# Ordering the 128 partitions of layer 1's tiles channel first in a two-layer convolution kernel

## The chip, the cores and the metric

The kernel runs on one core of one Trainium2 chip. The metric is device microseconds (us) of one execution, the median of several runs. A core has a matrix engine (PE; its weight loads are written PEld), a vector engine (DVE), an activation engine (ACT), a general engine (POOL) and a queue that issues transfers (SP). Each runs its own instruction stream in order and waits on semaphores that the others raise. Transfers (DMA) are issued by SP here and carried by 16 DMA engines.

## What is computed

Two layers on a batch of 32 images of 96 channels, 56 by 56 pixels. Layer 0 is a 7x7 depthwise convolution, a layer norm over channels, a two-layer MLP with GELU and a residual; the change leaves it alone. Layer 1, cut to what matters:

```python
x = conv5x5_depthwise(x) + conv_b;  xs = silu(x)               # (B, 96, L), L = 56*56
dts, Bs, Cs = split(einsum('kd,bdl->bkl', x_proj_w, xs))       # 6, 4 and 4 rows
delta = softplus(einsum('dr,brl->bdl', dt_w, dts) + dt_b)
log_dA = maximum(delta * -exp(A_logs), log(1e-9))              # for each of N = 4 states
P = exp(cumsum(log_dA, axis=-1))
hs = P * cumsum(delta * Bs * xs / maximum(P, 1e-9), axis=-1)
y = einsum('bdnl,bnl->bdl', hs, Cs) + xs * Ds
```

## The kernel before

The images are worked in 8 groups of `GI` = 4. Layer 0 runs over all groups and stores its result in `x1`; then layer 1 runs over them. In layer 1 a tile of 128 partitions holds 4 images by `CB` = 32 channels, and three tiles (t = 0, 1, 2) hold the 96 channels of a group. The pixels of an image are cut into 7 bands of `BT` = 448. A group has 7 bands x 3 tiles x 4 states = 84 steps s. In each step DVE runs two scans along the pixels (`scan_q` L1082, `scan_h` L1109) with a product between them (`gate`, L1098), POOL makes `u` (`times_b`, L1000) and `h` times C (`times_c`, L1010 and L1013), ACT makes `d_a` for five steps ahead (L1189, L1195), and PE adds the result to the bank `ps_y` (`add_y`, L1380). The first of the four states of a tile is preceded by the product of `xs` and `skip` (L1377), which opens `ps_y` anew.

All through the group the front of the next group is worked between these steps, one unit at a time: "turn" (PE turns a strip of `x1pad`, L1300), "conv" (PE multiplies windows with the banded filter in `taps`, L1307) and "back" (PE turns `conv` back so that channels and images are the partitions, L1320). ACT keeps each unit's bank: `keep_front`, L1145, into `win` or `conv`, and `silus`, L1152, into `xs`. The front of a group has 192/8 = 24 conv units, each with one filter load `taps` of 672 KB. ACT's copies for one conv unit write 4 channels x 4 images x 28 row pairs to 112 partitions of `conv`.

When a tile's four states are in `ps_y`, ACT copies them to `y` (`keep_y`, L1215), at step 4k + 6, and SP stores `y` to the output (`store`, L932) at step 4k + 7. There is one tile `y` and one bank `ps_y`. So `keep_y` waits for the tile's last product on PE and for the whole landing of the store before (`y_stored`), and PE's L1377 of the next tile waits for `keep_y`:

```python
act.wait_ge(y_added, g * S + (r + 1) * N + H_SLOTS)
act.wait_ge(y_stored, (g * RUNS + r + 1) * 16)
nc.scalar.activation(y[:, :], ps_y[:, 0:BT], ACT.Copy).then_inc(y_kept, 1)
```

SP's order is written out in `group`: for each step first the loads due in 5 steps (`load_slab` L906 into `x1pad`, `load_taps` L915, each of which waits until PE is done with its slot), then the store. Also on each other's way are `spread_b` (PE, L1350) and `keep_b` (ACT, L1203), which make `b_rows` of the next band in steps 6 to 10 of a band, `softplus` (ACT, last part L1171), and `sum_delta` (DVE, L1072), which waits for it. `lay_out` on the host orders the weights that go with the partitions.

Of the kernel before, what the change touches and what calls it, by code (L numbers as in the profile page):

```python
# [28 lines left out]
ds = bass.ds  # L29

IMAGES, C, H, W = 32, 96, 56, 56
L = H * W
GI = 4
# [37 lines left out]
CB = 32  # L71
# [648 lines left out]
def layer1(nc, groups, x1, t2, consts, out):  # L720

    x1img = x1.rearrange("r (h w) -> r h w", h=H)
    with ExitStack() as ctx:  # L723
        def sb(name, shape, dt=F32):
            return ctx.enter_context(nc.sbuf_tensor(name, shape, dt))
# [23 lines left out]
        conv = sb("conv2", [TOK, IMG_BLK, GI * C])  # L749
# [139 lines left out]
        @block.sync  # L889
        def _(sp):  # L890
            sp.dma_start(ident[:, :], consts["ident"]).then_inc(ident_in, 16)
            small = [(xproj[:, :, :], consts["xproj"]),
                     (xs[:, 0, 0:2 * 128], consts["sel"]),
                     (xs[:, 1, 0:TILES * 128], consts["dtw"]),
                     (ds_col[:, :], consts["ds"]),
                     (conv_bias[:, :], consts["cb2"]), (low_rows[:, :], consts["low_rows"]),
                     (a_neg[:, :, :], consts["a_logs"])]

            def load_slab(f, first, k):

                if k >= SLABS:
                    sp.wait_ge(front_done, f * FRONT + turn_unit[k - SLABS] + 1)
                elif not first:
                    sp.wait_ge(front_done, (f - 1) * FRONT + turn_unit[k - SLABS] + 1)
                rows = slice(CB * (k % SLABS), CB * (k % SLABS) + CB)
                sp.dma_start(xpad[rows, PAD2:PAD2 + H, PAD2:PAD2 + W],  # L906
                             x1img[ds((f * GI + k % GI) * C + CB * (k // GI), CB), :, :]
                             ).then_inc(slab_ready[k % SLABS], 16)

            def load_taps(f, first, k):  # L910
                if k >= SLOTS2:
                    sp.wait_ge(front_done, f * FRONT + conv_unit[k - SLOTS2] + 1)
                elif not first:
                    sp.wait_ge(front_done, (f - 1) * FRONT + conv_unit[k - SLOTS2] + 1)
                sp.dma_start(taps[k % SLOTS2][:, :, :, :], t2[k]).then_inc(taps_ready[k % SLOTS2], 16)  # L915


            loads = [(load_slab, k, turn_unit[k] - TURNS2 + 1) for k in range(CBS * GI)]
            loads += [(load_taps, k, conv_unit[k]) for k in range(QUNITS)]
            loads.sort(key=lambda load: load[2])  # L920

            sp.wait_ge(xpad_zero, BORDERS)
            for n, (load, k, _) in enumerate(loads):
                if n == SLABS:
                    for dst, src in small:
                        sp.dma_start(dst, src).then_inc(consts_in, 16)
                load(0, True, k)

            def store(g, r):
                b, t = r // TILES, r % TILES  # L930
                sp.wait_ge(y_kept, g * RUNS + r + 2)
                sp.dma_start(out.rearrange("(i c) l -> i c l", c=C)[ds(g * GI, GI), t * CB:(t + 1) * CB,  # L932
                                                                    b * BT:(b + 1) * BT],
                             y[:, :]).then_inc(y_stored, 16)

            def first_slabs(f):
                for load, k, _ in loads[:SLABS]:
                    load(f, False, k)

            def group(g, ahead):  # L940

                todo = loads[SLABS:] if ahead else []
                for s in range(S):
                    if ahead == 2 and s == S - 2 * STEPS:
                        first_slabs(g + 2)
                    while todo and unit_step[todo[0][2]] <= s + AHEAD:
                        load, k, _ = todo.pop(0)
                        load(g + 1, False, k)
                    if s >= N + Y_LAG + 1 and (s - N - Y_LAG - 1) % N == 0:
                        store(g, (s - N - Y_LAG - 1) // N)  # L950
                store(g, RUNS - 1)

            if last:
                first_slabs(1)
            if last > 1:
                with sp.Fori(0, last - 1) as g:
                    group(g, 2)
            if last:
                group(last - 1, 1)
            group(last, 0)  # L960
            sp.wait_ge(y_stored, (groups * RUNS + 1) * 16)
# [171 lines left out]
        def _(act):  # L1133
            def keep_front(f, i):

                kind, cb, k, p = units[i]
                act.wait_ge(front_done, f * FRONT + i + 1)
                if kind == "turn":
                    src = bank[i][0:WIN2, 0:TW2 * CB].rearrange("p (w c) -> p w c", c=CB)
                    dst = win[cb % 2][:, :, k, p * TW2:(p + 1) * TW2].rearrange("p c w -> p w c")  # L1140
                else:
                    src = bank[i][0:TOK, 0:CQ * BLOCKS].rearrange("p (c i b) -> p c i b", c=CQ, i=GI)
                    dst = conv[:, :, cb * 128:(cb + 1) * 128].rearrange("p b (i c) -> p c i b",
                                                                        i=GI)[:, k * CQ:(k + 1) * CQ, :, :]
                nc.scalar.activation(dst, src, ACT.Copy).then_inc(front_kept, 1)  # L1145

# [107 lines left out]
            for i in range(EARLY):  # L1254
                if units[i][0] != "back":
                    keep_front(0, i)
                elif units[i - 1][0] != "back":
                    silus(0, next(burst for burst in backs if i in burst))
# [181 lines left out]
def banded(w, k):  # L1440

    cols = W + k - 1
    kt = (ROWS + k - 1) // ROWS
    t = np.zeros((C, kt * ROWS, cols, ROWS, W), np.float32)
    for o in range(ROWS):
        for j in range(W):
            t[:, o:o + k, j:j + k, o, j] = w
    t = t.reshape(QUNITS, CQ, kt, ROWS * cols, TOK).transpose(0, 3, 1, 2, 4)
    return np.pad(t, ((0, 0), (0, 128 - ROWS * cols), (0, 0), (0, 0), (0, 0)))


def lay_out(i):

    image, channel = np.divmod(np.arange(128), CB)

    def rows(a):

        a = a.reshape((TILES, CB) + a.shape[1:]).swapaxes(0, 1)
        return np.ascontiguousarray(np.tile(a, (GI,) + (1,) * (a.ndim - 1)))

    xproj = np.zeros((128, TILES, XD), np.float32)
    dtw = np.zeros((XD, TILES, 128), np.float32)
    sel = np.zeros((XD, 2, 128), np.float32)
    low_rows = np.zeros((XD, 2), np.float32)
    low_rows[ONE, 1] = 1
    weights = i["L1_conv_x_proj_w"]
    for part in range(2):
        for t in range(TILES):
            for p in range(128):
                m, c = image[p], t * CB + channel[p]  # L1470
                for n in range(N):
                    for k in range(2):
                        row = n * XB + (2 * part + k) * GI + m
                        xproj[p, t, row] = weights[R + k * N + n, c]
                        sel[row, k, p] = 1
                        low_rows[row, 0] = part
                dts = m * XB + DT0 + part * R
                xproj[p, t, dts:dts + R] = weights[:R, c]
                dtw[dts:dts + R, t, p] = i["L1_conv_dt_w"][c]
                low_rows[dts:dts + R, 0] = part  # L1480
                dtw[ONE, t, p] = i["L1_conv_dt_b"][c]
    return {
        "x": i["x"], "t1": banded(i["L0_conv_conv_w"][:, 0], K1), "ident": np.eye(128, dtype=np.float32),
        "w1": i["L0_conv_w1"], "w2": i["L0_conv_w2"], "b1": np.ascontiguousarray(i["L0_conv_b1"].reshape(FT, 128).T), "b2": i["L0_conv_b2"],
        "ln_g": i["L0_conv_ln_g"], "ln_b": i["L0_conv_ln_b"], "ls": i["L0_conv_layer_scale"].reshape(C),
        "cb1": i["L0_conv_conv_b"],
        "t2": banded(i["L1_conv_conv_w"][:, 0], K2),
        "xproj": xproj, "dtw": dtw.reshape(XD, -1), "sel": sel.reshape(XD, -1), "low_rows": low_rows,
        "ds": rows(i["L1_conv_Ds"]), "cb2": rows(i["L1_conv_conv_b"]),
        "a_logs": rows(i["L1_conv_A_logs"]),  # L1490
    }

# [19 lines left out]
```

## Time and profile before

| | us |
|---|---|
| median of 3 runs (4328.0 to 4345.21) | 4344.35 |
| the profiled execution | 4339.02 |
| its span on the core | 4337.2 |
| layer 1, from its first loads at 1845 | 2492 |

The profile is one execution of the program. Busy time of an engine says how long it worked; a wait names the instruction that waited and the one whose semaphore ended the wait. `PEclk` is the clock granted to the matrix engine: 1.00 is 2.4 GHz and 0.50 is 1.2 GHz. In the timeline a row gives the start, the duration, the engine, the line and the tiles, and in brackets the idle time of the engine ahead of it with what ended it. Buffer numbers are left out of the tiles' names.

### The profile page before, as it was taken

The numbers are of one execution on the slowest core, as the hardware profiler recorded it, in microseconds if no ns is written. First come the engines' busy times: TensorE is split into PE (matmuls) and PEld (weight loads), VectorE is DVE, ScalarE is ACT, GpSimd is POOL, SyncE is SP. The second block draws the span as 40 slices with busy tenths as digits, with TensorE's granted clock in tenths as the row PEclk, the third lists the DMA queues.
The fourth block names the chain that finished last, engine by engine and source line by source line (L and its number), as shares of the span: only waits on it lengthen the run. The fifth ranks groups of instructions, "written<-read, shape, count | busy, mean of one in ns | idle before, by whom it ended". The sixth has DMA issues, their size and how long they took to land. (4 is left out here: it accounts for less than half of the span.)

```text
span 4337.2 us, 74817 instructions
## 1 busy us (share of the span) xinstructions
PE 3832.3 (88%) x22806; PEld 2788.2 (64%) x22806; DVE 3180.4 (73%) x4643; ACT 2788.1 (64%) x4796; POOL 2363.8 (55%) x2504
## 2 busy tenths in 40 slices
PE   7999999999999999977888889888888888898777
PEld 6787888878787878675555545545545555455432
DVE  3767667676758585705977978878878778788898
ACT  1545445453637272747877877878778778778875
POOL 0323223232314141405877868777868778777798
PEclk9999999999999999988997978979979979889977
DMA  7565555546464744274423324424324334243100
GB/s 233 146 181 155 168 165 155 174 136 193 120 213 99 237 101 165 74 186 90 107 73 92 103 55 108 109 56 104 102 59 109 81 78 112 62 102 97 39 20 22
DMA packets 314885, 507.50 MB, mean 117 GB/s; under 512 B 190000, under 2 KB 255248, under 8 KB 314144
## 3 DMA queue, kind: packets, MB, share of 16 engines
q1 hardware_dynamic: 314432, 502.08, 42.3%
q8 instruction: 209, 3.42, 0.3%
q14 instruction: 244, 2.00, 0.2%
HBM read 424.94 MB, written 77.07 MB: 116 GB/s over the span
## 5 line engine op out<-in xcount | busy, mean ns | idle before, releaser
L522 ACT ACTIVATE act_h<-ps_up,b 128x448 f32<-128x448 f32 x672 | 408.4, 633 | 789.1 <-PE ps_up L640 788.9
L1013 POOL TENSOR_TENSOR h<-h,c_rows 128x448 f32<-128x448 f32 x672 | 762.9, 1135 | 103.8 <-ACT c_rows L1210 53.3
L319 POOL TENSOR_TENSOR h_low<-act_h,h_high 128x448 fp32r<-128x448 f32 x224 | 287.2, 1282 | 902.0 <-ACT h_high L527 901.9
L1000 POOL TENSOR_TENSOR u<-dxs,b_rows 128x448 f32<-128x448 f32 x672 | 763.9, 1137 | 27.0 <-ACT b_rows L1203 20.4
L1380 PE MATMUL ps_y<-h,ident 128*128 128x448 f32 x1344 | 725.5, 627 | 42.5 <-POOL h L1013 32.1
L1082 DVE TENSOR_TENSOR_SCAN ps_q<-d_a,q_last,ps_q 128x448 f32<-128x448 f32 x576 | 659.6, 1145 | 25.2 <-ACT d_a L1195 25.2
L1109 DVE TENSOR_TENSOR_SCAN h<-d_a,h_last,ps_q 128x448 f32<-128x448 f32 x576 | 645.7, 1121 | 9.7 <-PE ps_y L1380 9.6
L1307 PEld LDWEIGHTS ps_front<-win,taps 120*112 120x112 f32 x4608 | 537.8, 188 | 137.5 <-issue 136.5
L613 PE MATMUL ps_stage<-win,taps 124*112 124x112 f32 x6144 | 607.9, 260 | 2.7 <-DVE w_low L366 2.7
L613 PEld LDWEIGHTS ps_stage<-win,taps 124*112 124x112 f32 x6144 | 607.7, 178 | 3.3 <-DVE w_low L366 2.8
L1307 PE MATMUL ps_front<-win,taps 120*112 120x112 f32 x4608 | 550.1, 273 | 5.4 <-ACT win L1145 3.7
L1098 DVE SCALAR_TENSOR_TENSOR ps_q<-ps_q,u 128x448 f32<-128x448 f32 x672 | 422.4, 629 | 160.7 <-POOL u L1000 137.3
L1189 ACT ACTIVATE d_a<-delta,log_eps,a_neg 128x448 f32<-128x448 f32 x672 | 505.5, 753 | 50.0 <-DVE h L1109 33.1
L314 POOL TENSOR_TENSOR ln_rstd<-ln_var,minus_half 112x7 f32<-112x7 f32 x128 | 244.7, 1912 | 406.8 <-DVE ln_var L401 406.8
L429 DVE TENSOR_TENSOR conv<-ps_stage,bias_row 112x448 f32<-112x448 f32 x192 | 180.0, 937 | 350.2 <-PE ps_stage L613 350.2
L1380 PEld LDWEIGHTS ps_y<-h,ident 128*128 128x128 f32 x1344 | 249.0, 209 | 243.7 <-issue 168.6
L1195 ACT ACTIVATE d_a<-d_a 128x448 f32<-128x448 f32 x672 | 384.5, 573 | 2.7
L1377 PE MATMUL ps_y<-xs,skip 128*128 128x448 f32 x336 | 196.6, 672 | 194.0 <-ACT y L1215 193.6
L1072 DVE SCALAR_TENSOR_TENSOR delta<-ps_prep,z_log 128x448 f32<-128x448 f32 x168 | 104.2, 620 | 293.0 <-ACT z_log L1171 289.1
L1145 ACT ACTIVATE conv<-ps_front 112x448 f32<-112x448 f32 x192 | 181.8, 947 | 173.8 <-PE ps_front L1307 173.6
L636 PE MATMUL ps_up<-hn_high,w_high 96*128 96x448 f32 x672 | 254.6, 379 | 35.2 <-DVE hn_low L411 20.3
L1300 PEld LDWEIGHTS ps_front<-ident,x1pad 32*120 32x120 f32 x2880 | 209.0, 151 | 116.9 <-issue 115.3
(93 smaller groups left out, 7118.2 us busy)
## 6 DMA issues: line engine op xcount, KB each, us to landing
taps<-in_t_dram SPq DMA_DIRECT2D x192, 896.0 KB, 5.2
taps<-in_t_dram SPq DMA_DIRECT2D x192, 672.0 KB, 4.8
xres<-in_x_dram SPq DMA_DIRECT2D x224, 168.0 KB, 2.5
x_dram<-x1o SPq DMA_DIRECT2D x224, 168.0 KB, 2.0
x1pad<-x_dram SPq DMA_DIRECT2D x96, 392.0 KB, 8.0
out_dram<-y SPq DMA_DIRECT2D x168, 224.0 KB
xpad<-in_x_dram SPq DMA_DIRECT2D x29, 1176.0 KB, 10.6
conv<-in_x_dram SPq DMA_DIRECT2D x3, 1176.0 KB, 15.3
```

Source lines behind the costliest of these rows:

```text
L319: nc.gpsimd.tensor_tensor(h_low[u % 2][:, 1, :], act_h[u % 2][:, 1, :], h_high[u % 2][:, 1, :], ALU.subtract).then_inc(h_low_ready[1], 1)
L522: nc.scalar.activation(act_h[u % 2][:, t, :], ps_up[t][:, 0:BT], ACT.Gelu, bias=b1[:, t:t + 1]).then_inc(gelu_done, 1)
L613: mm = nc.tensor.matmul(ps_stage[q % 2][0:TOK, c * BLOCKS:(c + 1) * BLOCKS], taps[q % SLOTS1][0:WIN1, c, k, :], win[:, q * CQ + c, :, k:k ...
L1000: nc.gpsimd.tensor_tensor(u[s % U_SLOTS][:, :], dxs[:, t, :], b_rows[n][:, :], ALU.mult).then_inc(u_done, 1)
L1013: nc.gpsimd.tensor_tensor(h[s % H_SLOTS][:, :], h[s % H_SLOTS][:, :], c_rows[n][:, :], ALU.mult).then_inc(hc_done, 1)
L1082: nc.vector.tensor_tensor_scan(ps_q[s % 2][:, 0:BT], d_a[s % DA_SLOTS][:, :], no_q.broadcast_to([128, BT]), first, ALU.mult, ALU.add).then ...
L1098: nc.vector.scalar_tensor_tensor(ps_q[s % 2][:, 0:BT], ps_q[s % 2][:, 0:BT], 1.0, u[s % U_SLOTS][:, :], ALU.min, ALU.mult).then_inc(gated, 1)
L1109: nc.vector.tensor_tensor_scan(h[s % H_SLOTS][:, :], d_a[s % DA_SLOTS][:, :], ps_q[s % 2][:, 0:BT], first, ALU.mult, ALU.add).then_inc(h_d ...
L1189: nc.scalar.activation(d_a[s % DA_SLOTS][:, :], delta[:, t, :], ACT.Relu, bias=log_eps[:, 0:1], scale=a_neg[:, t, n:n + 1]).then_inc(clipp ...
L1195: nc.scalar.activation(d_a[s % DA_SLOTS][:, :], d_a[s % DA_SLOTS][:, :], ACT.Exp, bias=LOG_EPS).then_inc(d_a_ready, 1)
L1307: mm = nc.tensor.matmul(bank[i][0:TOK, c * BLOCKS:(c + 1) * BLOCKS], taps[n % SLOTS2][0:WIN2, c, w, :], win[cb % 2][:, k * CQ + c, :, w:w ...
L1380: nc.tensor.matmul(ps_y[:, 0:BT], ident[:, :], h[s % H_SLOTS][:, :], start=False, stop=(n == N - 1)).then_inc(y_added, 1)
```

## The change

The 128 partitions of a layer 1 tile were ordered image first (partition = 32 image + channel); now channel first (partition = 4 channel + image). ACT's copy L1145 writes `conv` in that order, the host lays the weights out to match, and the store of `y` has 32 leading entries (channels) of 4 images in place of 4 leading entries (images) of 32 channels. The store's source is the same `y[:, :]` of 128 partitions, its pieces are the same 448 pixels (1,792 bytes), and it moves the same 224 KB.

```diff
             def store(g, r):
                 b, t = r // TILES, r % TILES
                 sp.wait_ge(y_kept, g * RUNS + r + 2)
-                sp.dma_start(out.rearrange("(i c) l -> i c l", c=C)[ds(g * GI, GI), t * CB:(t + 1) * CB,
+                sp.dma_start(out.rearrange("(i c) l -> c i l", c=C)[t * CB:(t + 1) * CB, ds(g * GI, GI),
                                                                     b * BT:(b + 1) * BT],
                              y[:, :]).then_inc(y_stored, 16)
...
-                    dst = conv[:, :, cb * 128:(cb + 1) * 128].rearrange("p b (i c) -> p c i b",
+                    dst = conv[:, :, cb * 128:(cb + 1) * 128].rearrange("p b (c i) -> p c i b",
                                                                         i=GI)[:, k * CQ:(k + 1) * CQ, :, :]
...
-    image, channel = np.divmod(np.arange(128), CB)
+    channel, image = np.divmod(np.arange(128), GI)
...
-        return np.ascontiguousarray(np.tile(a, (GI,) + (1,) * (a.ndim - 1)))
+        return np.ascontiguousarray(np.repeat(a, GI, axis=0))
```

No instruction is added, taken away or moved on any engine. On SP, at steps 61 to 67 of a group (sixth band), the queue stood as follows before; `taps2_0` to `taps2_2` are the three slots of the filter tile, `ISA` and `REGISTER_ALU` are address and semaphore work.

```order
L915 DMA taps2_0<-in_t2_dram 128x1344
L912 REGISTER_ALU
L915 DMA taps2_1<-in_t2_dram 128x1344
L931 REGISTER_ALU
L932 ISA
L932 DMA out_dram<-y 4x32x448
L912 REGISTER_ALU
L915 DMA taps2_2<-in_t2_dram 128x1344
```

The same place in the changed kernel:

```order
L915 DMA taps2_1<-in_t2_dram 128x1344
L931 REGISTER_ALU
L932 ISA
L932 DMA out_dram<-y 32x4x448
L912 REGISTER_ALU
```

The order is the same; only the shape of the store has moved from 4x32x448 to 32x4x448. On ACT the copy of a conv unit changes its shape and nothing else:

```order
-L1145 ACTIVATE conv<-ps_front 112x4x4x28
+L1145 ACTIVATE conv<-ps_front 112x16x28
```

Channels and images, apart before, now lie next to each other in `conv` and fold into 16; the innermost 28 row pairs are 384 elements apart in both.

## Rows read from the trace of the kernel before

**Rows 1.** The page, part 1: busy time, share of the span, instructions.

```profile
PE 3832.3 (88%) x22806; PEld 2788.2 (64%) x22806; DVE 3180.4 (73%) x4643; ACT 2788.1 (64%) x4796; POOL 2363.8 (55%) x2504
```

**Rows 2.** Waits, 2010 to 4130 us: waiting <- releaser: total us, times, longest.

```profile
PE ps_y L1377 <- ACT y L1215: 164.4, 135, 3.8
...
ACT y L1215 <- DMA out_dram<-y: 11.6, 7, 2.2
```

**Rows 3.** Timeline of steps 61 to 68 of the third group: start, duration, instruction.

```profile
2811.02 6.68 SPq L915 DMA_DIRECT2D taps<-in_t_dram  x2
2817.95 0.64 SPq L932 DMA_DIRECT2D out_dram<-y  x1
...
2824.68 0.54 ACT L1215 ACTIVATE y<-ps_y 128x448 f32<-128x448 f32 x1 [1.73 <-DMA out_dram<-y]
...
2825.36 1.83 PE L1377 MATMUL ps_y<-xs,skip 128*128 128x448 f32 x2 [3.31 <-ACT y L1215]
...
2830.86 0.56 PE L1350 MATMUL ps_bc<-parts,sel 32*128 32x448 f32 x1
...
2831.46 0.54 ACT L1203 ACTIVATE b_rows<-ps_bc 128x448 f32<-128x448 f32 x1 [4.08 <-PE ps_bc L1350]
...
2832.16 1.14 POOL L1000 TENSOR_TENSOR u<-dxs,b_rows 128x448 f32<-128x448 f32 x1 [0.79 <-ACT b_rows L1203]
...
2833.12 0.62 DVE L1072 SCALAR_TENSOR_TENSOR delta<-ps_prep,z_log 128x448 f32<-128x448 f32 x1 [5.20 <-ACT z_log L1171]
...
2835.92 0.19 POOL L1010 TENSOR_TENSOR h_last<-h,zeros 128x1 f32<-128x1 f32 x1 [2.62 <-DVE h L1109]
```

**Rows 4.** Timeline of ACT: the first and the last of the seven waits.

```profile
2226.18 0.54 ACT L1215 ACTIVATE y<-ps_y 128x448 f32<-128x448 f32 x1 [2.09 <-DMA out_dram<-y]
...
4025.21 0.54 ACT L1215 ACTIVATE y<-ps_y 128x448 f32<-128x448 f32 x1 [0.78 <-DMA out_dram<-y]
```

**Rows 5.** Timeline of POOL behind the first and the last wait.

```profile
2236.36 0.19 POOL L1010 TENSOR_TENSOR h_last<-h,zeros 128x1 f32<-128x1 f32 x1 [2.62 <-DVE h L1109]
...
4035.34 0.19 POOL L1010 TENSOR_TENSOR h_last<-h,zeros 128x1 f32<-128x1 f32 x1 [1.34 <-DVE h L1109]
```

**Rows 6.** Windows: from:to, length, busy of PE, PEld, DVE, ACT, POOL, PEclk, DMA share, GB/s.

```profile
2825.00:2831.00 6.00, 5.64 (x17) 3.80 (x17) 2.89 (x5) 2.35 (x5) 5.84 (x8) 0.50 0.17 49
2840.00:2850.00 10.00, 7.78 (x44) 5.38 (x45) 10.00 (x12) 7.54 (x13) 9.81 (x10) 1.00 0.09 23
4025.00:4031.00 6.00, 5.10 (x18) 3.14 (x19) 4.33 (x7) 2.79 (x6) 5.84 (x8) 0.72 0.37 130
```

**Rows 7.** Timeline of PE at two shorter stalls.

```profile
2868.21 1.02 PE L1377 MATMUL ps_y<-xs,skip 128*128 128x448 f32 x2 [1.45 <-ACT y L1215]
...
3168.71 1.59 PE L1377 MATMUL ps_y<-xs,skip 128*128 128x448 f32 x2 [1.46 <-ACT y L1215]
```

**Rows 8.** Windows, the 5 us behind each of these two stalls.

```profile
2868.20:2873.20 5.00, 4.96 (x13) 2.11 (x13) 5.00 (x7) 4.79 (x10) 5.00 (x6) 1.00 0.18 48
3168.70:3173.70 5.00, 4.99 (x9) 1.94 (x9) 5.00 (x7) 3.20 (x7) 5.00 (x6) 0.66 0.18 48
```

**Rows 9.** DMA issues: count, KB each, median us from issue to landing.

```profile
x_dram<-x1o SPq DMA_DIRECT2D x224, 168.0 KB, 2.0
x1pad<-x_dram SPq DMA_DIRECT2D x96, 392.0 KB, 8.0
```

**Rows 10.** SP's own waits, 4300 to 4338 us: for the last store, once issued.

```profile
SPq L723 <- DMA out_dram<-y: 4.6, 1, 4.6
```

**Rows 11.** DMA packets, 4322 to 4331 us: one store of `y` alone, and 8 KB instructions.

```profile
DMA packets 133, 0.24 MB, mean 26 GB/s; under 512 B 4, under 2 KB 132, under 8 KB 132
```

**Rows 12.** DMA packets, 1843 to 1847 us: one store of `x1o` and one load.

```profile
DMA packets 256, 0.24 MB, mean 59 GB/s; under 512 B 32, under 2 KB 256, under 8 KB 256
```

**Rows 13.** Groups of ACT by form, 2010 to 4130 us: busy us, mean ns, idle before.

```profile
L1145 ACT ACTIVATE win<-ps_front 120x480 f32<-120x480 f32 x167 | 178.1, 1066 | 114.9 <-PE ps_front L1300 114.9
L1145 ACT ACTIVATE conv<-ps_front 112x448 f32<-112x448 f32 x168 | 159.1, 947 | 130.5 <-PE ps_front L1307 130.3
```

## The prediction, on record before the changed kernel ran

> **What bounds the kernel now.** I read the page's busy times first: PE is busy 88% of the span, DVE 73% [rows 1]. No engine is full, so a shorter transfer pays only where somebody waits for it and where that somebody holds up the rest. The change touches one transfer, the store of `y`, and one ACT copy. So the second view is the list of waits over the steady part of layer 1. PE waits 164.4 us for ACT's copy of `y`, in 135 places; ACT itself waits for the store of `y` in 7 places, 11.6 us together [rows 2]. The first number looks large, but it is mostly ACT's own order of work. Only the 11.6 us are the store's.
>
> There are seven groups with a next group to prepare, and each has one such wait, at its 67th step: the first is 2.09 us, the last 0.78 [rows 4]. The timeline of the third shows how it comes about [rows 3]. SP issues two filter loads ahead of the store, and the second had to wait for PE, so the store goes out at 2817.95, behind 672 KB just issued. It lands at 2824.68, where ACT's copy can start 1.73 us late. PE has been idle 3.31 us by then.
>
> **Whom that holds up.** Behind PE's stall come the two products into `ps_y`, a conv unit, and then the product L1350 at 2830.86. ACT had waited 4.08 us for it to make `b_rows`. The same ACT stream makes `z_log`, for which DVE had waited 5.20 us, and POOL, which had work stored up, runs dry last: 0.79 us for `b_rows` and 2.62 us for DVE's scan [rows 3]. A little later DVE and POOL are full, 10.00 and 9.81 of 10 us from 2840 on [rows 6], and PE is not. So PE is on the path through the stall, and POOL's idle time, 3.41 us here, is what a quicker PE could give back at most. Behind the seven waits these sums are 2.62, 3.68, 3.41, 3.65, 3.25, 3.23 and 1.34 us, 21.2 together (third in [rows 3], first and last in [rows 5]).
>
> **The clock.** A stall costs PE more than its length. In the 6 us after the stall the granted clock is 0.50, that is 1.2 GHz; behind the last one, where PE stood for 2.37 us, it is 0.72, a mix of both levels [rows 6]. The first pair of products takes 1.83 us after the stall [rows 3] and 1.02 where the clock held [rows 7]. Without the wait for the store all seven stalls would be 1.6 us long (3.31 less 1.73 here). The trace has two stalls nearly that long at another step: 1.45 us, after which the clock stayed at 1.00, and 1.46 us, after which it was 0.66 over 5 us [rows 7, 8]. At 1.6 us both can happen.
>
> **The store.** How many DMA engines carry it can be counted. A transfer ends with small packets that raise the semaphore. The last stores of the program lie alone: 128 packets of data and 4 below 512 bytes [rows 11]. In the other window a store of `x1o` (96 rows) and a load of 128 rows of 512 bytes leave 256 - 96 - 128 = 32 small ones, 16 each [rows 12]. So the store of `y` runs on 4 engines and the others on 16. With 32 leading entries I expect 16. What 32 entries do is not in this trace in so many packets.
>
> The Trainium skill ("DMA: Bandwidth & Descriptors", section on why a DMA increments its semaphore by 16) says that the number of engines is the largest up to 16 that divides the slowest dimension of both sides; for 4 against 128 that gives 4, as the trace has it, and for 32 against 128 it gives 16. By that rule the change does what it says.
>
> Price: SP waited 4.6 us for the last store [rows 10]. The nearest transfer on 16 engines is that of `x1o`, 2.0 us for 168 KB [rows 9]. For 224 KB the bounds are 2.0 (all of it fixed) and 2.7 (2.0 x 224/168, all of it by size), so a store lands 1.9 to 2.6 us earlier. Each engine then has 8 rows instead of 32 behind the filter load. I take 2.2.
>
> **The sum, part by part.**
> - End of the program: nothing hides the last store, 2.2 us less.
> - The waits of ACT: three of the seven are above 1.9 us (2.09, 2.17, 2.09). At 2.2 saved all 11.6 go; at 1.9, 11.0. In the other stores nobody waits for the landing, and they give nothing: ACT does not come back before four steps, some 14 us.
> - The clock behind the stalls. If every place became like the last one, with the short low clock and no wait (POOL would still idle 1.34 - 0.78 = 0.56 us there), the seven give 21.2 - 7 x 0.56 = 17.3 us, the 11.6 included. If the clock stays as it is, 11.6. If it never falls, all of POOL's idle time, 21.2.
> - The ACT copy into `conv`: 947 ns for 448 elements. The copy into `win`, also with no two neighbours written in turn, takes 1066 ns for 480, 2.2 ns an element against 2.1 [rows 13]. Innermost are 28 elements 384 apart before and after; only the outer steps swap. I take nothing. The bounds are 30 ns either way, 168 x 0.03 = 5 us if all of it lay on the path, about half of it in truth, since ACT idles 130.5 us ahead of these copies.
> - Loads: a filter or `x1pad` load behind a store comes in earlier on four engines, but the list of waits has none of PE for a load in this stretch. Nothing. PE's products sum the same values over permuted partitions: same shapes, nothing.
> - SP: issue of the store takes 0.64 us [rows 3]; SP has slack, nothing.
>
> Forecast: 17.3 less 0.5 for what stays of the longest waits, and 2.2 at the end: 19 us. The profiled execution took 4339.0, so it becomes 4320. It lies 5.3 us under the median of the runs, 4344.35; the same 19 us from there give **4325 us**, 0.44% less. About 0.5% (21.7 us) is what a measurement of this kernel can tell from no change.
>
> **The rivals.**
> 1. *The clock falls as before.* A stall of 1.6 us still brings the full low stretch. Then 11.3 + 2.2 = 13.5 us: 4331. For it: the stall of 1.46 us was already enough once [rows 8]. Against: 2.37 us brought a shorter stretch than 3.31 [rows 6].
> 2. *The clock never falls there.* 21.2 - 0.5 + 2.2 = 23 us: 4321. For it: the stall of 1.45 us [rows 7, 8]. Against: 1.6 is longer.
> 3. *Nothing moves.* The store stays on 4 engines, or its landing at these seven places is set by the filter loads ahead of it on all engines, so that it comes no earlier. 4342 to 4344. For it: the store goes out right behind 672 KB [rows 3]. Against: engines work their own share in order, and a quarter of the rows on each is less behind the same load.
> 4. *Slower.* An engine's rows, neighbouring channels 12.5 KB apart in the output before, are now four images 1.2 MB apart. If such writes are slow, the store lands later. The nearest transfer of scattered pieces, `x1pad` with 8.0 us [rows 9], is 3.4 us above 4.6. Then each of the seven waits grows by 3.4 and so does the end: 8 x 3.4 = 27 us, 4371. It decides from no gain at all per store; the 0.5% are reached at 2.7 us more per store. Against: most of the 8.0 us are 1,792 small pieces, and a store of `y` has 128.
>
> On that the Trainium skill ("DMA: Bandwidth & Descriptors", section on latency and other measured facts) lists that copies whose rows lie 2, 4 or 8 MiB apart, powers of two, run at down to half the rate, and that a pitch off by 4 KiB restores it. Here the pitch is 1,204,224 bytes, no power of two; by that page the store would not suffer, and no run so far shows it.
>
> **How the numbers follow.** Forecast 0.38, rival 1 0.20, rival 2 0.18, nothing 0.12, slower 0.07; 0.05 for a larger gain, if the groups' falls of the clock elsewhere shift in our favour. The three runs before lie 17 us apart, so each case has some 8 us about it. The range 4308 to 4345 takes in the cases from the larger gain to no effect, and leaves out rival 4 and the far tails. Faster by over 0.5% holds rival 2 in good part, the larger gain and the better side of the forecast: 0.33. Within 0.5%: 0.59. Slower: 0.08.
>
> **What would show each step.** The lone store at the end: 16 small packets, not 4, and SP's last wait 2.0 to 2.7 us. The wait of ACT for the store: gone, or a few tenths in three places. PE's stalls at these steps: 1.6 us each; the clock in the 6 us behind them at 0.7 or above (0.5 speaks for rival 1, 1.0 for rival 2). POOL's idle time there: about 0.6 us. The period of a group, 300 us between two such copies, goes to 297.5. The copy into `conv`: 947 ns still. The forecast is wrong if POOL or DVE turns out to be held by something else behind the stall, if the copy's time moves by more than 30 ns, or if the store does not come in earlier.

## The result

| | median us | runs |
|---|---|---|
| before | 4344.78 | 4328.0 to 4349.79 |
| changed kernel | 4284.92 | 4279.36 to 4288.19 |

The ratio is 0.9867 with a 95% interval from 0.9846 to 0.9889: 60 us less where 19 were forecast, and below the range of 4308 to 4345. The profiled execution took 4279.36 us, against 4339.02 before.

The transfer itself did what was expected. The lone store of `y` near the end, from the DMA packets of the changed kernel between 4262 and 4272 us (before: [rows 11]), and SP's own last wait (before: [rows 10]):

```profile
DMA packets 146, 0.25 MB, mean 25 GB/s; under 512 B 16, under 2 KB 144, under 8 KB 144
```

```profile
SPq L723 <- DMA out_dram<-y: 1.8, 1, 1.8
```

16 small packets close the store instead of 4: it runs on 16 engines. SP waits 1.8 us for the last one instead of 4.6, a little less than the 2.0 to 2.7 that I had given. The page's list of DMA issues (count, KB, median us to landing; [rows 9] answers to the second line) shows that the loads land earlier too; the filter loads took 4.8 us before:

```profile
taps<-in_t_dram SPq DMA_DIRECT2D x192, 672.0 KB, 4.0
x1pad<-x_dram SPq DMA_DIRECT2D x96, 392.0 KB, 5.3
out_dram<-y SPq DMA_DIRECT2D x168, 224.0 KB, 2.4
```

ACT's waits at `keep_y` fell from 11.6 us in 7 places [rows 2] to this line of the view of L1215 (what ended ACT's idle time, us, times):

```profile
  DMA out_dram<-y: 0.2, 1
```

**Where the 60 us arise.** The starts of ACT's copies of `y` mark the steps of each group. Cut at steps 14, 58 and 74, the fourth group reads so in the windows of the kernel before (columns as in [rows 6]):

```profile
2949.60:3089.70 140.10, 124.07 (x763) 82.89 (x762) 126.99 (x186) 119.04 (x206) 119.85 (x145) 0.99 0.41 105
3089.70:3159.80 70.10, 60.05 (x296) 40.92 (x296) 51.70 (x71) 51.54 (x86) 44.70 (x53) 0.85 0.34 81
3159.80:3249.90 90.10, 76.88 (x313) 42.15 (x312) 65.31 (x92) 64.39 (x110) 64.62 (x71) 0.73 0.28 69
```

and in the changed kernel:

```profile
2927.70:3067.80 140.10, 124.10 (x763) 82.92 (x762) 127.24 (x188) 119.04 (x206) 119.83 (x145) 0.99 0.38 105
3067.80:3131.50 63.70, 55.50 (x298) 37.88 (x298) 51.14 (x70) 51.20 (x87) 44.55 (x53) 0.95 0.38 89
3131.50:3214.40 82.90, 67.59 (x312) 36.34 (x310) 65.53 (x90) 63.66 (x110) 64.55 (x72) 0.81 0.29 75
```

The long first stretch is the same to the tenth. DVE, ACT and POOL have the same work in all three. In the second stretch (steps 58 to 74, the *site* of the wait) 6.4 us are gone, and in the third (step 74 to step 14 of the next group, the *turn*) 7.2. In both the granted clock is higher, 0.95 for 0.85 and 0.81 for 0.73, and PE's busy time shorter with the same matmuls. Over the seven groups the sites take 450.6 us instead of 486.3, 36 less. The turns of the first six take 515.3 instead of 542.6, 27 less. The end gives 3, and 6 are lost again in the seventh turn, the middles and the first steps.

Within the site the fourth group reads as follows, cut at the copies of `y` at steps 62, 66, 70 and 74, before:

```profile
3112.10:3125.40 13.30, 9.61 (x63) 7.30 (x62) 6.71 (x11) 9.93 (x18) 10.29 (x13) 0.97 0.52 166
3125.40:3140.40 15.00, 13.91 (x64) 9.51 (x64) 9.46 (x15) 10.97 (x21) 11.03 (x15) 0.80 0.07 22
3140.40:3159.80 19.40, 16.78 (x74) 10.62 (x74) 16.86 (x21) 15.27 (x25) 11.15 (x11) 0.82 0.05 13
```

and after:

```profile
3090.10:3101.10 11.00, 9.60 (x63) 7.30 (x62) 4.45 (x7) 9.70 (x18) 8.08 (x10) 1.00 0.46 152
3101.10:3113.50 12.40, 11.30 (x64) 7.87 (x64) 11.69 (x18) 10.97 (x21) 12.09 (x16) 1.00 0.19 70
3113.50:3131.50 18.00, 14.77 (x76) 9.23 (x76) 16.29 (x20) 15.01 (x26) 12.12 (x13) 1.00 0.04 14
```

The wait itself gives 2.3 us. The stretches behind it, where the clock now holds at 2.4 GHz, are 2.6 and 1.4 us shorter. (The 0.95 of the whole site comes from steps 58 to 62, where the clock is 0.85 in both kernels.) PE's stall in the fourth group before, and the timeline of the changed kernel at the place of [rows 3], one group on:

```profile
3126.10 1.83 PE L1377 MATMUL ps_y<-xs,skip 128*128 128x448 f32 x2 [3.68 <-ACT y L1215]
```

```profile
3096.31 0.62 SPq L932 DMA_DIRECT2D out_dram<-y  x1
...
3101.12 0.57 ACT L1215 ACTIVATE y<-ps_y 128x448 f32<-128x448 f32 x1
...
3101.83 0.99 PE L1377 MATMUL ps_y<-xs,skip 128*128 128x448 f32 x2 [1.41 <-ACT y L1215]
...
3105.19 0.54 ACT L1203 ACTIVATE b_rows<-ps_bc 128x448 f32<-128x448 f32 x1 [1.35 <-PE ps_bc L1350]
...
3106.85 0.62 DVE L1072 SCALAR_TENSOR_TENSOR delta<-ps_prep,z_log 128x448 f32<-128x448 f32 x1 [0.57 <-ACT z_log L1171]
```

PE stands for 1.41 us instead of 3.68 and its pair takes 0.99 instead of 1.83 us. DVE's wait is 0.57 instead of 5.44, and POOL does not idle there any more. Six of the seven groups look like this one. In the first, PE still stands for 1.83 us, the clock behind it is 0.72 and the site takes 68.3 us.

### The profile page after: what moved, and what is told of

Same layout as the page of the kernel before. It is cut to its first block and busy times, and to the rows that moved or that the text cites. A ratio compares the mean times of both kernels' runs of the same rounds, so it can differ in the third digit from the quotient of the medians.

```text
span 4277.6 us, 74817 instructions
## 1 busy us (share of the span) xinstructions
PE 3785.7 (89%) x22806; PEld 2758.0 (64%) x22806; DVE 3180.8 (74%) x4643; ACT 2783.8 (65%) x4796; POOL 2363.1 (55%) x2504
## 5 line engine op out<-in xcount | busy, mean ns | idle before, releaser
L1307 PEld LDWEIGHTS ps_front<-win,taps 120*112 120x112 f32 x4608 | 527.1, 185 | 134.4 <-issue 132.6
L1307 PE MATMUL ps_front<-win,taps 120*112 120x112 f32 x4608 | 539.5, 269 | 6.1 <-ACT win L1145 3.7
L1145 ACT ACTIVATE conv<-ps_front 112x448 f32<-112x448 f32 x192 | 181.7, 946 | 166.0 <-PE ps_front L1307 165.8
```

Source lines behind the costliest of these rows:

```text
L1307: mm = nc.tensor.matmul(bank[i][0:TOK, c * BLOCKS:(c + 1) * BLOCKS], taps[n % SLOTS2][0:WIN2, c, w, :], win[cb % 2][:, k * CQ + c, :, w:w ...
```

## The experiments

The theory after the result: the shorter landing of the store takes away ACT's wait at step 66; that keeps PE's stall so short that its clock holds, and most of the gain is the clock. Rivals: the order of partitions itself brings the gain; or the relief of four DMA engines, by earlier loads; or each us of wait simply costs a us; and for the turn, that its gain is not the store's at all. The table gives medians, beside the kernel before on the same chip, and the site and turn of the profiled execution (mean of seven sites, range of the first six turns).

| kernel | us | before | ratio, 95% interval | site us | turns us |
|---|---|---|---|---|---|
| changed kernel | 4284.9 | 4344.8 | 0.9867 (0.9846 to 0.9889) | 64.4 | 82.9 to 89.4 |
| img_4x16 | 4295.7 | 4339.9 | 0.9889 (0.987 to 0.9909) | 64.3 | 83.0 to 90.5 |
| img_2x2 | 4336.2 | 4339.9 | 0.999 (0.9976 to 1.0004) | 70.6 | 83.2 to 91.2 |
| store_first | 4276.3 | 4339.9 | 0.984 (0.9823 to 0.9856) | 64.3 | 83.0 to 90.4 |
| chan_4x8 | 4284.2 | 4339.9 | 0.9868 (0.9836 to 0.99) | 63.8 | 82.8 to 90.5 |
| delay66_4 | 4283.6 | 4347.7 | 0.9847 (0.9808 to 0.9887) | 63.7 | 87.2 to 90.8 |
| delay66_8 | 4310.6 | 4347.7 | 0.9918 (0.9888 to 0.9948) | 66.8 | 83.1 to 90.7 |
| delay66_12 | 4322.2 | 4341.4 | 0.9955 (0.9939 to 0.997) | 66.1 | 90.2 to 90.4 |
| delay30_8 | 4271.9 | 4347.7 | 0.9831 (0.9801 to 0.986) | 63.5 | 82.9 to 90.2 |
| delay74_2 | 4286.5 | 4341.4 | 0.9875 (0.9844 to 0.9906) | 64.7 | 82.7 to 90.3 |
| before_d74_1 | 4346.3 | 4338.5 | 1.0006 (0.9987 to 1.0026) | 68.7 | 90.2 to 90.4 |
| before_d74_3 | 4339.7 | 4338.5 | 1.0008 (0.9997 to 1.0019) | 68.6 | 83.0 to 90.2 |
| before_d74_6 | 4335.1 | 4338.5 | 0.9999 (0.998 to 1.0018) | 69.1 | 83.1 to 90.8 |
| before_y_first | 4255.6 | 4341.4 | 0.9793 (0.9762 to 0.9823) | 66.6 | 80.0 to 82.5 |
| y_before_front | 4225.1 | 4347.7 | 0.9727 (0.9693 to 0.9761) | 64.3 | 77.6 to 82.6 |
| both_first | 4206.4 | 4341.4 | 0.9689 (0.9661 to 0.9718) | 61.7 | 79.7 to 83.3 |

The kernel before has 69.5 and 90.1 to 90.9 in these columns. Its own medians lie up to 9 us apart between these sets of runs, so kernels of different rows are best compared by their ratios.

### Layout or landing: img_4x16

Image first as before, with four transfers per store:

```diff
-                sp.dma_start(out.rearrange("(i c) l -> i c l", c=C)[ds(g * GI, GI), t * CB:(t + 1) * CB,
-                                                                    b * BT:(b + 1) * BT],
-                             y[:, :]).then_inc(y_stored, 16)
+                for i in range(GI):
+                    sp.dma_start(out[ds((g * GI + i) * C + t * CB, CB), b * BT:(b + 1) * BT],
+                                 y[i * CB:(i + 1) * CB, :]).then_inc(y_stored, 16)
```

> The kernel before with its image-first partitions, but each store of y issued as four transfers, one per image, each with 32 leading entries. Theory S (the shorter landing of the store makes the difference, by way of ACT's wait at the 67th step and PE's clock behind it): small packets per store 64, all 16 engines busy; landing 1.5 us after that of the changed kernel because of three more issues of 0.55 us; ACT's waits for the store nearly gone; 4285 us, give or take 8. Theory L (the channel-first order itself makes it, by ACT's copy or the weights): 4345.

4295.7 us, with the sites at 64.3 us. The page's issues (columns as above):

```profile
out_dram<-y SPq DMA_DIRECT2D x672, 56.0 KB, 1.6
```

So most of the gain is there without the new order of partitions: 44 us of 60, and at the sites all of it. Its ratio, 0.9889, is not clear of the 0.9867 of the changed kernel, since the intervals overlap. What its profiled execution lacks lies at the turns and in the first steps. The order of partitions is only the means by which one transfer gets 32 leading entries.

### Eight engines: chan_4x8

The changed kernel, with four transfers of 8 channels each:

```diff
-                sp.dma_start(out.rearrange("(i c) l -> c i l", c=C)[t * CB:(t + 1) * CB, ds(g * GI, GI),
-                                                                    b * BT:(b + 1) * BT],
-                             y[:, :]).then_inc(y_stored, 16)
+                for k in range(4):
+                    sp.dma_start(out.rearrange("(i c) l -> c i l", c=C)[t * CB + 8 * k:t * CB + 8 * k + 8,
+                                                                        ds(g * GI, GI), b * BT:(b + 1) * BT],
+                                 y[32 * k:32 * k + 32, :]).then_inc(y_stored, 16)
```

> The changed kernel with its channel-first partitions, but each store of y issued as four transfers of 8 channels, with 8 leading entries each, so that 16 rows lie on each of 8 engines. Theory S: landing between before and after (0.6 us more than on 16 engines, 1.7 us more for the issues); ACT's waits 0 to 3 us in all; 4285 to 4300. Theory L: 4285.

4284.2, the changed kernel's time. ACT's waits for the store:

```profile
ACT y L1216 <- DMA out_dram<-y: 0.7, 2, 0.4
```

Half the engines do as well as all, since nobody waits for the rest of the landing. This run does not tell the theories apart by itself; with img_4x16 it says that any landing short enough at step 66 will do.

### Two engines: img_2x2

```diff
+                for k in range(2):
+                    sp.dma_start(out.rearrange("(i c) l -> i c l", c=C)[ds(g * GI + 2 * k, 2), t * CB:(t + 1) * CB,
+                                                                        b * BT:(b + 1) * BT],
+                                 y[64 * k:64 * k + 64, :]).then_inc(y_stored, 16)
```

> The kernel before, but each store of y issued as two transfers of two images, with 2 leading entries each, so that 64 rows lie on each of two engines instead of 32 on each of four. Theory S: a store lands some 2.4 us later still than before (32 more rows of 74 ns, read off the lone store's rows); ACT's waits for it grow from 11.6 us to 28 or more, and the time goes up by 10 to 40 us, 4355 to 4385. Theory L, or that the landing is of no matter: 4345.

The waits grew as said, but the time did not: 4336.2, within the noise of before. ACT's waits, and PE's stall in the fourth group:

```profile
ACT y L1216 <- DMA out_dram<-y: 30.5, 12, 4.2
```

```profile
3111.46 1.83 PE L1378 MATMUL ps_y<-xs,skip 128*128 128x448 f32 x2 [5.83 <-ACT y L1216]
```

A miss of my forecast, and the clearest sign against "a us of wait costs a us": of the 19 us more of waiting some 15 lie at the seven sites, and they lengthen them by 8 us together (3.4 are one wait at the end of a group), and the turns, 83 to 91 us, give that back. Behind stalls of 4.7 to 5.8 us the clock of the next 6 us is 0.65 to 0.74, where it was 0.50 to 0.56 behind five of the seven stalls of before; so the longer stall is in part paid back right behind it.

### The wait alone: store_first

Four leading entries as before; only SP's list is turned:

```diff
+                    if s >= N + Y_LAG + 1 and (s - N - Y_LAG - 1) % N == 0:
+                        store(g, (s - N - Y_LAG - 1) // N)
                     while todo and unit_step[todo[0][2]] <= s + AHEAD:
                         load, k, _ = todo.pop(0)
                         load(g + 1, False, k)
-                    if s >= N + Y_LAG + 1 and (s - N - Y_LAG - 1) % N == 0:
-                        store(g, (s - N - Y_LAG - 1) // N)
```

> The kernel before with 4 leading entries, but in SP's list the store of a step stands ahead of the loads of that step. No transfer is quicker; the store of the 64th step is issued some 5.6 us earlier, since it no longer waits behind a filter load. Theory S in the form that only the wait matters: ACT's waits for the store are gone, 4285 give or take 10. If instead the relief of the four engines is what counts (filter and image loads landing earlier), the time stays at 4345, and their landings stay at 4.8 and 8.0 us.

4276.3, no slower than the changed kernel, with loads that land later than in any other kernel but img_2x2 (6.1 and 8.7 us), and PE's stall in the fourth group:

```profile
taps<-in_t_dram SPq DMA_DIRECT2D x192, 672.0 KB, 6.1
x1pad<-x_dram SPq DMA_DIRECT2D x96, 392.0 KB, 8.7
```

```profile
3105.43 0.99 PE L1377 MATMUL ps_y<-xs,skip 128*128 128x448 f32 x2 [1.42 <-ACT y L1215]
```

This settles it between the wait and the load on the four engines. The quick landing is not needed; it is enough that the store does not stand behind a filter load on SP.

### Putting the wait back: delay66_4, delay66_8, delay66_12

The changed kernel with n tiny copies ahead of the copy of `y` at step 66. One takes about 0.18 us, but they overlap: four take 0.43 us in all, eight 0.82 and twelve 1.19. With eight:

```diff
+                    if more and s == 66:
+                        for k in range(8):
+                            nc.scalar.activation(ps_bc[:, BT + 8 * k:BT + 8 * k + 8], skip[:, 0, 0:8], ACT.Copy)
```

> The changed kernel with four of the tiny ACT copies at step 66, some 0.8 us. Theory C: PE's stall is 2.2 us, as long as the shortest of before; the clock falls behind it, 4300 to 4330. Theory linear: 7 x 0.8 = 6 us, 4291.

> The changed kernel with eight tiny ACT copies (8 elements each, some 0.2 us, into unused columns of a bank) ahead of the copy of y at step 66 of every group but the last. They stand in for the wait for the store: no transfer is touched. Theory C (the wait costs mostly by what PE's clock does behind it, there and at the turn of the group): most of the 60 us come back, 4325 to 4345, PE's stall 3 us and the granted clock 0.5 to 0.7 in the 6 us behind it. Theory linear (a us of wait costs a us): 7 x 1.6 = 11 us, 4296.

> The changed kernel with twelve tiny ACT copies (5 elements each) at step 66, where eight had brought PE's stall from 1.41 to 2.12 us and a fall of the clock behind it. Theory C: the stall is 2.8 us and the clock low for longer; the stretch from step 58 to 74 takes 69 to 70 us as in the kernel before (63.7 in the changed one, 66.9 with eight), and the whole 4310 to 4345. Theory linear: 66.9 plus 0.7.

The timelines of PE in the fourth group, in this order, with the window of the 6 us behind it for each:

```profile
3102.68 0.99 PE L1380 MATMUL ps_y<-xs,skip 128*128 128x448 f32 x2 [1.74 <-ACT y L1215]
```

```profile
3103.00:3109.00 6.00, 6.00 (x35) 4.07 (x34) 5.04 (x9) 4.63 (x10) 5.84 (x8) 1.00 0.24 96
```

```profile
3109.03 1.70 PE L1380 MATMUL ps_y<-xs,skip 128*128 128x448 f32 x2 [2.12 <-ACT y L1215]
```

```profile
3109.00:3115.00 6.00, 5.96 (x21) 3.61 (x22) 3.71 (x7) 2.94 (x7) 5.84 (x8) 0.72 0.21 81
```

```profile
3107.35 1.83 PE L1380 MATMUL ps_y<-xs,skip 128*128 128x448 f32 x2 [2.49 <-ACT y L1215]
```

```profile
3107.40:3113.40 6.00, 6.00 (x24) 3.62 (x25) 3.28 (x5) 3.08 (x7) 5.84 (x8) 0.74 0.15 59
```

The stall of 1.74 us costs nothing: the clock stays at 1.00 in all seven groups, and the median is that of the changed kernel. The stall of 2.12 us, 0.4 longer, brings the clock down in all seven: each site takes 3.1 us more than with 1.74, the whole 27 us more. With 2.49 us it is 4322, still 19 us below before. No transfer was touched, so an ACT delay alone brings back about 26 and 37 of the 60 us by the medians, 22 and 38 by the ratios. The three medians move by steps, not in proportion to the delay. Expected sizes were off: the copies add less to the stall than I had reckoned (0.33, 0.71 and 1.08 us), four cost less than either theory said, eight gave less than "most of the 60", and the site did not reach 69 us with twelve. Nor does the loss lie only at the sites: with twelve copies the seven sites give back 12 us, and the first six turns, 90.3 us each, all 27.

### Another place: delay30_8

The same eight copies at step 30.

> The changed kernel with the eight tiny ACT copies ahead of the copy of y at step 30 instead, the same step of a band three bands earlier, where PE is as busy. Theory C for any place: PE's stall there is 2.7 us, the clock falls behind it, 4310 to 4345. Theory linear or that only step 66 is tender: 4285 to 4296.

4271.9, 13 us *below* the changed kernel, though the intervals of the two ratios overlap. PE's stall at step 30 in the first and in the fourth group:

```profile
2102.61 1.86 PE L1380 MATMUL ps_y<-xs,skip 128*128 128x448 f32 x2 [2.06 <-ACT y L1215]
```

```profile
2973.47 1.02 PE L1380 MATMUL ps_y<-xs,skip 128*128 128x448 f32 x2 [2.05 <-ACT y L1215]
```

Without the copies this stall is 1.26 to 1.28 us long, so the eight bring it to 2.05 to 2.07 us, not to the 2.7 that I had reckoned with. Behind it the clock stays at 1.00 in six groups and falls to 0.73 in the first. The middle stretch takes 140.1 or 140.2 us in those six, no more than without the copies, so 0.8 us more of stall cost nothing there. Whether step 66 is more tender than step 30 is not shown by this: the stall here is shorter than the 2.12 us at which the clock fell in every group.

### The turns: delay74_2 and three kernels on the old store

One to six tiny copies at step 74, in the changed kernel (2) and in the kernel before (1, 3, 6), where the wait for the store is left as it was:

```diff
+                    if more and s == 74:
+                        for k in range(3):
+                            nc.scalar.activation(idle[:, 3 * k:3 * k + 3], skip[:, 0, 0:3], ACT.Copy)
```

> The changed kernel with two tiny ACT copies (8 elements, 0.3 us together) at step 74, where the turn of the group begins. Theory C for the turn (its time, 83 to 90 us from step 74 to step 14 of the next group, hangs on where PE's idle times fall against the steps of its clock, and not on the store): the turns take 83 to 90 us in another order than in the changed kernel, and the median lies anywhere from 4265 to 4300. If the turn's gain comes from the store: 83 to 88 us as before it, 4285.

> The kernel before, store and all, with one tiny ACT copy (3 elements, 0.18 us) at step 74, where the turn of the group begins. Question: the changed kernel's turns (step 74 to step 14 of the next group) take 83 to 89 us, those of the kernel before 90 us each time. Theory P (the turn depends on where its idle times fall against the clock, and the kernel before is caught in one pattern): turns leave 90 us in some groups, and the time is 0 to 30 us below before though work was added. Theory T (the turn is longer because of the wait at step 66 or the store): turns of 90 us, 4341 to 4345.

> The kernel before with three tiny ACT copies (0.5 us) at step 74. Theory P: turns anywhere from 83 to 91 us, 4305 to 4345. Theory T: turns of 90 us, 4345.

> The kernel before with six tiny ACT copies (1.1 us) at step 74. Theory P: turns anywhere from 83 to 91 us, 4305 to 4350. Theory T: turns of 90 us and 7 us more in all, 4350.

Medians of 4286.5, and of 4346.3, 4339.7 and 4335.1 against 4338.5: on average nothing moved. In delay74_2 the turns take 82.7 to 90.3 us in another order than in the changed kernel, as theory C for the turn has it. With one copy in the kernel before they stay at 90.2 to 90.4 us, as theory T has it. But the profiled execution of before_d74_3, the fastest of its eleven (4312.7), has two neighbouring groups whose turns are short. Windows, turn of the second group, then middle, site and turn of the third:

```profile
2550.60:2633.60 83.00, 67.40 (x311) 36.35 (x310) 65.18 (x90) 63.70 (x111) 64.43 (x71) 0.81 0.31 74
2633.60:2773.80 140.20, 124.18 (x763) 82.95 (x762) 127.34 (x188) 119.12 (x207) 119.93 (x145) 0.99 0.41 105
2773.80:2843.70 69.90, 60.08 (x296) 41.02 (x296) 51.64 (x70) 51.94 (x90) 44.69 (x53) 0.85 0.33 81
2843.70:2927.20 83.50, 68.54 (x313) 36.67 (x312) 64.98 (x91) 63.73 (x110) 64.43 (x71) 0.82 0.31 74
```

A site with the full wait, 69.9 us, is followed by a turn of 83.5. So a short turn does not need the store's wait gone (theory T falls in its strict form), and store_first has a turn of 90.4 without the wait. Yet the two are not independent. Over the first six groups of the fourteen profiled kernels that keep ACT's order, the turn takes 89.0 us on average behind the 26 sites longer than 69 us, 88.2 behind 21 sites of 65 to 68.5, and 86.4 behind the 37 shorter ones. That would be 2.6 x 6 = 16 us of the 27. It is a comparison across kernels and no test: delay66_4 has short sites and turns of 89.1 us in the mean. The medians say more. All five kernels in which PE's stall at step 66 stays short, and which are alike otherwise (changed, img_4x16, chan_4x8, store_first, delay66_4), lie 44 to 64 us below the kernel before, more than the 38 us that sites and end give; the three with copies at step 74 and the old store lie within 8 us of it. So more than the sites' share comes with the short stall at step 66. How it gets from step 66 to the turn, and which idle time decides between a turn of 83, 86, 88 or 90 us, stays open.

### A version that beats both: y_before_front, before_y_first, both_first

PE's waits for ACT's copy of `y` were still 151.8 us. In `group` of ACT the copy of `y` now stands ahead of the front's copy:

```diff
+                    if s >= N + Y_LAG and (s - N - Y_LAG) % N == 0:
+                        keep_y(g, (s - N - Y_LAG) // N)
                     if more:
                         for i in kept_at[s]:
                             keep_front(g + 1, i)
-                    if s >= N + Y_LAG and (s - N - Y_LAG) % N == 0:
-                        keep_y(g, (s - N - Y_LAG) // N)
```

> The changed kernel with ACT's copy of y ahead of the copy of the front unit's bank in the same step, so that PE gets ps_y back about 1 us earlier (the copy of a conv unit takes 0.95 us). Theory C: PE's stalls at L1377, 1.1 to 2.0 us each and 152 us in all, shrink by half, and with the shortest idle stretches gone the clock holds: 4200 to 4260. Against: the copy of y can then wait for PE's last product and hold up the front's bank, or POOL is the bound in these steps: 4275 to 4295.

> The kernel before (image first, stores on 4 engines) with ACT's copy of y ahead of the copy of the front's bank. It is due earlier, so it runs into the store before more often: the wait at step 66 grows by the 0.95 us of the conv unit's copy, to 2 to 3 us, and the clock falls behind it. 4290 to 4310, 65 to 85 us above the same edit on the changed kernel (4225). If the store's landing did not matter, it would come to 4225 as well.

> The changed kernel with both orders turned: on ACT the copy of y ahead of the front's copy, on SP the store ahead of the loads of its step. The first alone gave 4225. With the store issued up to 6 us earlier at step 64, no wait for it is left there either: 4205 to 4225. If none was left already: 4225.

The first is that edit on the changed kernel (4225.1), the second on the kernel before (4255.6), the third has store_first's edit besides (4206.4, a ratio of 0.9689, interval 0.9661 to 0.9718: 78 us below the changed kernel by the medians). The waits of the second and of the first, in this order:

```profile
PE ps_y L1377 <- ACT y L1215: 106.9, 98, 3.7
...
ACT y L1215 <- DMA out_dram<-y: 16.3, 7, 2.9
```

```profile
PE ps_y L1377 <- ACT y L1215: 100.5, 101, 2.9
...
ACT y L1215 <- DMA out_dram<-y: 6.0, 7, 1.8
```

The first falls in the range that I had given for it, but not in the way that theory C had it. PE's waits went from 151.8 to 100.5 us, a third less and not half. Nor does the clock hold better: over the whole execution it is 0.925, against 0.927 in the changed kernel. Its profiled execution has shorter middles (18 us in seven) and shorter turns (33 us in six), and sites of the same length.

`keep_y` comes earlier, so it meets the store again: 6.0 us even on 16 engines, none with the store issued first. The old store costs 30 us against the new one here, where I had expected 65 to 85. PE's stalls at step 66 with the old store are 2.5 to 3.7 us long, about as before, but the clock of the 6 us behind them is 0.72 to 0.74 in all seven groups and not down to 0.50; with the new store it is 0.72 in two groups and 1.00 in five. Why the same stall costs less clock here stays open. both_first came out at the lower end of what was expected.

## Why the prediction was wrong

**Right.** The chain [rows 3, 4] was the right one. The store moved from 4 to 16 engines; rival 3 falls, as does rival 4, with a landing of 2.4 us. The rule on the number of engines in the Trainium skill ("DMA: Bandwidth & Descriptors", section on why a DMA increments its semaphore by 16) gave 16 for 32 against 128 entries, and the 16 small packets agree. ACT's waits went from 11.6 to 0.2 us. The last wait of SP shrank by 2.8 us for the 2.2 taken. The copy into `conv` takes 946 ns in the mean for 947. The engines' work and the middle of the groups did not move.

**The stall.** I took 1.6 us for what would remain of PE's stall, from 3.31 less 1.73. It is 1.41, because ACT's copies overlap by about 0.2 us when nothing lies between them (in the fourth group the copy of the conv unit ends at 3101.31 and that of `y` starts at 3101.12), which the wait had hidden. At 1.6 I let both outcomes of the clock stand and chose a short fall. delay66_4 shows that it holds even after 1.74 us, and delay66_8 that it falls after 2.12. Of my cases rival 2 (the clock never falls there) was the true one in six groups of seven; I gave it 0.18. The two stalls of [rows 7, 8] had told more than I read from them: in the 6 us ahead of either PE was busy for 4.9 us at a clock of 1.00, the stalls are equally long, and yet the clock fell behind one alone. So the length of a stall, and the work just ahead of it, do not decide the clock by themselves.

**The cap.** The step that failed most is the term of the clock, which I closed with POOL's idle time, 21.2 us for the seven places [rows 3, 5]. As far as POOL's next steps go this was right: its 3.65 us of idle time in the fourth group are gone. But the sites gave 36 us. I ended the account where POOL was full [rows 6] and did not look at the steps after that. In the last stretch of the site POOL is busy for just 11.2 of 19.4 us in the kernel before and 12.1 of 18.0 in the changed one, so it capped nothing there. The clock in the kernel before falls once more between 3140 and 3160, when the back units start, and in the changed kernel it does not (0.82 against 1.00 in the windows above). So the term was 17.3 us and should have been 36.

**The turn.** It did not stand in the sum at all. Of the places where the clock of the kernel before is lowest, the turn of each group, at 0.73, I had no row, only a 0.05 for "falls of the clock elsewhere". It gave 27 us in the profiled execution. I had listed the engines' busy shares and the waits, and read the clock only at the seven places of the wait. The window of a whole group would have shown that most of the low clock lies in the turn (0.73 over 90 us, against 0.85 over 70 at the site); that it would move, nothing in the kernel before showed.

**Loads.** That they land earlier and that this gives nothing was right: store_first has slower loads than the kernel before and the time of the changed kernel.

The range was too narrow since it was built from the terms of the sum, all of which end at the place of the wait. Beyond the 0.05 nothing in it covered a second effect at another step. The chain of work and the direction were right; three times the forecast came from terms that the sum had too small or did not have.

## What to carry to other kernels

The slowest dimension of a store's access decided how many DMA engines carried it (4 leading entries, 4 small packets; 32 leading entries, 16); count the small packets that close a transfer lying alone. A transfer that somebody waits for may also be freed by its place in the queue: putting the store ahead of loads that wait for PE brought as much as four times the engines. When PE's clock is mixed, price a stall of a us or two over the whole period of the loop, at every stretch of low clock, and not only at its own place. Expect steps: here the first 0.33 us more of stall in each of seven groups cost nothing, and the next 0.38 us cost 27 us together.

## What was unexpected in the hardware

- At step 66, behind PE's stalls of up to 1.74 us, the clock stayed at 2.4 GHz; behind 2.08, 2.12, 2.49 and more it went to 1.2 GHz for a part of the next 6 us. In between it went either way: it fell behind 1.83 us in the changed kernel and 1.93 in chan_4x8, and held behind 1.84 in chan_4x8 and 1.92 in y_before_front. At step 30 it fell behind one of seven stalls of 2.05 to 2.07 us.
- Stalls of 2.4 to 3.8 us and of 4.7 to 5.8 us cost about the same: the sites of before and img_2x2 take 69.5 and 70.6 us in the mean.
- The turn takes from 82.7 to 91.2 us in the kernels that keep ACT's order, with a mean clock from 0.82 down to 0.71, though its instructions are the same but for the tiny copies. Up to six of these copies at its start in the kernel before made no turn longer than 90.8 us and some as short as 83.0.
